# Filler matmuls on TensorE in the long waits of a four-block mixer

## The reference

```python
x = x + L0(gn(x))   # deformable convolution: x1 = gelu(layernorm(dwconv3x3(x))),
                    # offset = x1 @ off_w, mask = softmax over 9 taps of (x1 @ mask_w),
                    # sum over taps of mask * bilinear sample of (x @ in_w), then @ out_w
x = x + L1(gn(x))   # routed Fourier filter: route = softmax over 4 filters of a pooled conv net,
                    # xp = relu(x @ w_pw1)**2, irfft2(rfft2(xp) * (route . spectra))
                    # + xp * (route2 . spatial), then @ w_pw2
x = x + L2(gn(x))   # linear attention with 5x5 depthwise taps on q, k, v, then a projection
x = x + L3(gn(x))   # depthwise 3x3, prune, 1x1 convolution, prune
```

## Time and profile before

| | us |
|---|---|
| median of 3 runs | 785.11 |
| lowest, highest | 783.10, 788.51 |
| the profiled execution | 790.58 |
| its span, first to last instruction | 788.80 |
| TensorE busy | 684.1 (87%) |
| VectorE busy | 533.2 (68%) |
| ScalarE busy | 327.8 (42%) |
| GpSimd busy | 339.2 (43%) |
| mean granted TensorE clock | 0.950 |

### The profile page before, as it was taken

The page is one execution under the profiler, slowest core; times in us unless marked ns, Lnnn a source line. Parts: engine busy times, 40 slices in busy tenths (PEclk is TensorE's granted clock), DMA queues, the critical chain, the costliest instruction groups (busy, mean ns, idle before and its releaser), DMA issues.

```text
span 788.8 us, 9014 instructions
## 1 busy us (share of the span) xinstructions
PE 684.1 (87%) x3532; PEld 368.9 (47%) x3532; DVE 533.2 (68%) x622; ACT 327.8 (42%) x486; POOL 339.2 (43%) x200
## 2 busy tenths in 40 slices
PE   1969889889877999999699999598989988989696
PEld 0655668789833654442211655243452324335232
DVE  5998979977472336001335223499999999995598
ACT  4725700020104340002354211269788969753263
POOL 6810049999605330000000000608999979950060
PEclk9989899999997999999779999799899999999989
DMA  5069200860019139402016400200000000000002
GB/s 189 1 94 146 29 0 1 126 121 9 1 51 293 56 124 342 174 0 107 11 70 213 134 1 1 84 0 1 1 1 1 1 1 1 1 1 0 14 1 106
DMA packets 37767, 49.53 MB, mean 63 GB/s; under 512 B 2644, under 2 KB 26004, under 8 KB 36396
## 3 DMA queue, kind: packets, MB, share of 16 engines
q1 hardware_dynamic: 37724, 48.94, 23.1%
HBM read 28.19 MB, written 10.49 MB: 49 GB/s over the span
## 4 chain that ended last, share of the span: by engine, by line
PE 54%; DVE 26%; POOL 8%; ACT 4%; issue 3%; DMA 3%; SPq 0%; DVEq 0%; POOLq 0%; ACTq 0%
DVE psum L421 13%; PE psum L897 8%; PE psum L835 5%; PE psum L1134 4%; PE psum L1007 4%; PE psum L868 3%; POOL arena L2102 3%; PE psum L1106 3%; PE psum L782 3%; PE psum L993 2%; PE psum L915 2%; PE psum L971 2%; POOL arena L2116 2%; PE psum L755 2%; PE psum L821 2%
## 5 line engine op out<-in xcount | busy, mean ns | idle before, releaser
L421 DVE SCALAR_TENSOR_TENSOR psum<-arena,psum 128x1024 f32<-128x1024 f32 x123 | 158.5, 1288 | 3.9
L2191 POOL TENSOR_TENSOR arena<-arena 128x1024 f32<-128x1024 f32 x76 | 151.4, 2029 | 10.9 <-ACT arena L1930 10.4
L835 PE MATMUL psum<-arena 128*128 128x128 f32 x800 | 93.7, 277 | 8.1 <-DVE arena L499 6.9
L835 PEld LDWEIGHTS psum<-arena 128*128 128x128 f32 x800 | 88.6, 142 | 13.1 <-DVE arena L499 8.9
L1930 ACT ACTIVATE arena<-arena 128x1024 f32<-128x1024 f32 x80 | 91.6, 1178 | 4.5 <-POOL arena L2191 4.4
L499 DVE TENSOR_TENSOR arena<-arena,psum 128x2048 f32<-128x2048 f32 x37 | 82.0, 2283 | 15.6 <-PE psum L835 7.0
L2150 POOL MEMSET arena<- 128x864 f32 x1 | 0.8, 836 | 201.1 <-DVE arena L1530 201.1
L1106 PE MATMUL psum<-arena 64*64 64x512 f32 x648 | 81.6, 617 | 2.2 <-ACT arena L1972 1.8
L897 PE MATMUL psum<-arena 128*128 128x512 f32 x144 | 63.8, 602 | 0.0
L499 POOL TENSOR_TENSOR arena<-arena 128x2048 f32<-128x2048 f32 x13 | 47.0, 3638 | 1.3 <-PE psum L835 1.2
L1022 PE MATMUL psum<-arena 128*128 128x512 f32 x96 | 43.0, 610 | 4.3 <-ACT arena L1711 4.3
(11 more groups left out here) (240 smaller groups left out, 1202.0 us busy)
## 6 DMA issues: line engine op xcount, KB each, us to landing
arena<-fc_w_dram SPq DMA_DIRECT2D x10, 1024.0 KB, 12.2
bounce<-arena SPq DMA_DIRECT2D x32, 256.0 KB, 2.0
arena<-bounce SPq DMA_DIRECT2D x32, 256.0 KB, 5.3
arena<-arena SPq DMA_DIRECT2D x16, 480.0 KB
arena<-x_dram SPq DMA_DIRECT2D x4, 512.0 KB, 5.1
out_dram<-arena SPq DMA_DIRECT2D x3, 512.0 KB, 2.6
arena<-sp_w_dram SPq DMA_DIRECT2D x1, 1152.0 KB
arena<-arena SPq DMA_DIRECT2D x8, 140.0 KB
```

The source lines that it names most:

```text
L421: return eng.scalar_tensor_tensor(dst, tap_view(t, a, b), wt, filter_acc, ALU.mult, ALU.add)
L835: m = pe.matmul(psum[:, 4 * hf + xx // 4, xx % 4 * P:(xx % 4 + 1) * P], prods[n % NB][:, xx * P:(xx + 1) * P], ident, start=(first and xx ...
L2191: g.tensor_tensor(dst, dst, tap_tmp(n), ALU.add).then_inc(s_ta, 1)
```

## The change

A helper `keep_clock(times, bank, width)` issues `times` matmuls with the identity as weights. What they stream, `filler`, are `width` columns of SBUF from the identity on: that is the identity itself and the two constants that lie behind it. They write over a PSUM bank that is not in use, and nothing reads their output. There are 53 of them, 49 of 384 columns and 4 of 256, at 14 places in TensorE's program. One wait is new, `pe.wait_ge(s_x_new, 1)` ahead of the second group norm. No other engine's program changes.

```diff
+        filler = words(top[0], 3 * P)
         ident = take(P)
         gmean = take(P)
         head_mask = take(P)
...
+            def keep_clock(times, bank, width=3 * P):
+
+                for n in range(times):
+                    pe.matmul(psum[:, bank, 0:width], ident, filler[:, 0:width], start=True, stop=True)
+
             pe.wait_ge(s_const, 80)
             group_means(0)
+            keep_clock(4, 3, 2 * P)
...
             sum_over_taps(0, 0, 12 * GH, SUM_BANKS[0])
             pe.wait_ge(s_ome, XX)
+            keep_clock(2, 7)
             pe.wait_ge(s_ones, 1)
             pe.wait_ge(s_amax, 1)
             pe.matmul(psum[:, 0, 0:1], ones, amax_all, start=True, stop=True).then_inc(s_om, 1)
+            keep_clock(1, 7)
             pe.wait_ge(s_exp, 7)
             sum_over_taps(0, 12 * GH, XG, SUM_BANKS[1])
+            keep_clock(2, 7)
             pe.wait_ge(s_exp, 8)
             sum_over_taps(1, 0, XG, SUM_BANKS[2])
+            keep_clock(3, 7)
             opened = set()
...
                 m.then_inc(s_wka, 1)
+            keep_clock(3, 3)
             pe.wait_ge(s_wd[0], 1)
...
+            pe.wait_ge(s_x_new, 1)
+            keep_clock(6, 0)
             group_means(1)
+            keep_clock(6, 0)
             pe.wait_ge(s_zc, 8)
             pe.wait_ge(s_w1, 64)
...
             for i in range(4, NS):
                 spectrum(i)
+            keep_clock(4, 3)
 
             pe.wait_ge(s_rd, 1)
...
             m.then_inc(s_rt, 1)
+            keep_clock(2, 3)
+
...
+            keep_clock(7, 0)
             group_means(2)
+            keep_clock(5, 0)
             pe.wait_ge(s_zc, 12)
...
+            keep_clock(4, 0)
             group_means(3)
+            keep_clock(4, 0)
             pe.wait_ge(s_zb, 3)
```

## The result

The changed kernel takes 776.10 us (median of 4, 773.80 to 780.18) against 785.75 us of before (median of 4): 9.65 us less, ratio 0.987 with a 95% interval of 0.983 to 0.991. The predicted time was 777. The profiled execution took 773.80 us, its span is 772.0 us, 16.8 less than the profiled one of before. So the two traces differ by far more than the medians, and not all of that is the work of the change.

A forecast was written before the change was run, and what follows sets the result against it. TensorE's half clock at waits was taken to cost time; 0.2 - 2.4 - 8.4 - 1.5 = -12.1 us gave 778.5 from the profiled 790.58, 773.0 from the median 785.11, weighted two to one: 777 us, range 772 to 785.5.

The forecast's parts named there:

- Price of a filler: TensorE: a filler of 384 columns takes 0.66 us, one of 256 takes 0.44 us, twice that at half clock.
- First norm 0: First group norm: four fillers, 1.75 us, fit in 3.69 us of wait, clock full anyway, so 0.
- Mask's softmax +0.2: Softmax sums: fillers do not fit, L821 starts 1.1 us later but runs at full clock, ending +0.2 us.
- Second norm -2.4: Second group norm: twelve fillers fit the waits, L854 saves half of 4.73 us at half clock, -2.4 us.
- Route -8.4: Route's softmax and tiles: clock kept, L961 starts 1.2 us earlier, steps take 2.56 us, together -8.4 us.
- Third norm -1.5: Third group norm: twelve fillers fit, L1022 at full clock lets VectorE's first tap start earlier, -1.5 us.
- Fourth norm 0: Fourth group norm: eight fillers fit the waits and the chain goes to VectorE, 0 either way.
- Rival 1: Clock falls at the route all the same, its term becomes +1.3 us, 783 us; chance 0.2.
- Rival 2: Mask's softmax loses its bet, the rest holds: 777 + 3.3 = 780 us; chance 0.12.
- Rival 3: Fillers' data does not hold the clock, fillers run at 1.31 us each, slower by over 1%; chance 0.09.
- Rival 4: More than summed: fall at 430 us goes too, or profiled execution is no worse at the route: 773; chance 0.1.
- Rival 5: All low clock was on the path, half of 51.4 us comes back: 759 us; chance 0.02.

The follow-up runs named there:

- fewer places: Whole change with fillers kept only at the route, second and third norm, plus two ahead of L843: 778.85 us, ratio 0.9898 to the kernel before.
- The route alone: Only the six fillers at the route's softmax (four, then two) kept from the whole change: 783.09 us, ratio 0.9947 to the kernel before.
- the one with too many: Whole change with eleven and nine fillers at the third group norm instead of seven and five: 779.55 us, ratio 0.9915 to the kernel before.
- the norms alone: Kernel before plus only the fillers at the second and third group norm (6 and 6, 7 and 5): 784.92 us, ratio 0.9966.

## Why the prediction was right

By its own steps:

- **Price of a filler.** 0.66 us; seven took 4.68 us as one block, right. (The first four, at half clock, took twice their price.)
- **First norm 0.** Wrong, and the one step that missed a gain. Its "the clock is full anyway" took the view's 1.00 for a measurement, when that view has no entry before 20.9 us; the 1.13 us of L741 in the earlier trace rows is its duration at half clock. The fillers fit, as forecast, but they also brought the clock up earlier: -1.02 us in the trace, -1.7 us between the medians of the traces with and without them. No run changed this place alone.
- **Behind L821: 0.** Right; a wait of 0.53 us is left of 2.47.
- **Mask's softmax +0.2.** The start of L821 moved by +0.5 us against the first sum, not by +1.1, because the small matmul took its place between fillers for 0.1 us and not 0.35, and sums behind a filler start without their latency. So -0.44 in the trace. But that compares with one execution of before. The same stretch was 133.77, 133.72, 133.64, 133.61, 132.51, 132.35 and 132.24 us in the seven traces without those fillers and 133.18 to 133.22 in the seven with them: no gain, only a fixed value. The step's conclusion was right.
- **Second norm -2.4.** L854 to L858 is 6.94 to 6.98 us in seven of eight traces with these fillers, against 8.58 to 9.38 in the six without: -1.6 to -2.4. Right, with the size at the upper end. In the eighth, the one shown above, the weights outlasted the fillers and it was 8.64; a wait of 2.32 us in the trace of fewer places did no harm.
- **Route -8.4.** The mechanism was right in each part: L938 1.92 us, the first L961 1.2 us earlier, steps of 2.56. Measured by stretch: -1.19 and -7.13. As a term of the median it was about twice too large. The route alone gave -4.2 us (-2.6 to -5.7). The profiled execution of before was at half clock for 20.5 us there, others without fillers for 10.2 and 13.6; and with fillers the last tiles fell in three traces of eight, which gives 1.4 to 3.6 us back. I had taken this variation as the reason to stay at 778.5 instead of 773.
- **Third norm -1.5.** 9.07 to 9.09 us in the traces with these fillers (but for the one with too many), 10.77 to 10.94 without: -1.7 to -1.9. Right.
- **Fourth norm 0.** Right, and by a stricter test than I had planned. Before the change this place had half clock too, a stretch that the prediction does not list:

```profile
748.00:754.70 6.70, 5.10 (x24) 1.70 (x28) 6.52 (x7) 5.81 (x6) 3.41 (x2) 0.50 0.00 0
```

With the fillers it is at 1.00, and the end is the same 39.04 us behind VectorE's first tap of the last block.

The reference point was the weak step. The sum of -12.1 us was right against the profiled execution (-0.44 - 2.32 - 1.19 - 7.13 - 1.71 = -12.8 at the same steps, -13.8 with the first norm), and wrong against the median, which moved by 9.65. 777 came out since I put two thirds of the weight on the first. That part of the route's half clock varies from run to run is borne out; the weight of two thirds is not, and that 777 lies within 1 us of 776.1 is partly luck. In the median the route gave 4.2 us less than its term, and the first norm's 1 to 2 us, which the sum did not have, made up for a part of it. Nor is the changed kernel free of the variation: its runs still spread over 6.4 us. The parts agree with the whole: the route alone gave -4.2 us, the norms alone -2.7, and the two with the fillers ahead of L843 -8.0 (-10.6 to -5.3).

Rival 1 (the route falls all the same) did not come with all six fillers, and did come with four. Rival 2's loss of 3.3 us did not come. Rival 3 is refuted: identity against constants, mostly zeros, holds the clock. Rival 4 named the fall at 430 us; it is gone in the first trace of the change and there in the second, so it is not removed but a matter of the execution. Rival 5 would have been 759 and did not come. The half clock on record, without the start, fell from 78.4 to 18.7 us between the two traces, and the spans by 16.8 us: TensorE's idle time and VectorE's 238 us don't shorten. The Trainium skill (TensorE: Matmul & The Clock Gate, Part 1, HAM oscillation) costs low clock at half its duration; the trace disagrees, since half of these 59.7 us would be 29.9. The five stretches of the prediction, 51.4 us, were not all there was: besides 748 us there were 51.6 to 58.4, 116.5 to 119.9 and 553.4 to 560.2.

My reading that 2.15 us of idle ahead of L843 does no harm was wrong. It was harmless in the trace I had. In 4 of the 11 traces without a filler there the clock fell behind it; a single trace shows what can happen at a gap, not that it does.

## What to carry to other kernels

Where TensorE waits a few microseconds and is the bound behind the wait, fill the wait with matmuls into a free bank, by count from their measured length, half a microsecond short of the wait; what sticks out is paid, here 3.0 us of 3.6. Look for the place where half clock lasts on while TensorE is busy, as the 20.5 us at the route, and cover every gap up to there. Where a view shows a full clock, compare the duration of one matmul with that of its like elsewhere: ahead of the clock's first entry the view says nothing. Before a term is taken from a profile, ask whether the thing it removes lasts the same in each execution; if not, the sum belongs to that execution's time and not to the median.

## What the runs showed of the hardware

- **The clock can stay down while TensorE works.** The tiles' mix ran at 1.2 GHz for 20.5 us with TensorE busy for 19.2 of them, and for 10.3 us with TensorE busy for 10.21 in the run with four fillers at the route. The same mix kept 2.4 GHz for up to 42.6 us once it had it (the route alone).
- **The same kernel falls or does not fall at the same gap.** The 2.15 us ahead of L843 were followed by a fall in 4 of 11 traces. Two executions of the changed kernel had 18.7 and 37.9 us at half clock, summed over their traces without the start, and spans 7.4 us apart.
- **TensorE started at half clock.** In all fourteen traces the first entry of the clock is 1.00, at 16.2 to 17.8 us in five of the six with fillers at the first norm (19.4 in the other) and at 20.5 to 23.5 us without. In the trace of before L741 took 1.06 us a record ahead of it and 0.60 behind it.
- **Transposes raised and held the clock like other matmuls.** In the trace of before the clock rose at 119.9 us, when only the transposes of L835 had run since 115.2, and stayed at 1.00 to 212 us; 33 transposes of the identity held it at the route.
- **Fillers of mostly zeros held it too**: of the 384 values that they streamed in each row 17 are not zero (the identity and two constants of 8 by 8 blocks), and the waits that they filled stood at 1.00 in the five stretches of the result.
